# A recurrence on one core: gate products in every step of a six-step loop, two transposes for one, and convolutions without dependent pairs

## The reference, cut to what matters

```python
def cell(h, x):
    gi = x @ W_ih + b_ih
    gh = h @ W_hh + b_hh
    i_r, i_z, i_n = jnp.split(gi, 3, axis=-1)
    h_r, h_z, h_n = jnp.split(gh, 3, axis=-1)
    r = jax.nn.sigmoid(i_r + h_r)
    z = jax.nn.sigmoid(i_z + h_z)
    n = jnp.tanh(i_n + r * h_n)
    h_new = (1.0 - z) * n + z * h
...
x = x + attention(x, cond)
x = x + gru(cond, x)
x = x + conv(x, w)         # w is cond, 4 taps
x = x + (conv(x, w) + b)
```

## Time and profile before

| | |
|---|---|
| median of three runs | 2157.09 us (2156.23 to 2157.23) |
| the profiled execution | 2157.61 us, span 2155.8 us |
| TensorE, matrix products busy | 2077.1 us, 96% |
| VectorE busy | 1391.0 us, 65% |
| ScalarE busy | 1173.3 us, 54% |
| GpSimd busy | 619.1 us, 29% |
| mean granted TensorE clock | 0.997 of full speed |

### The profile page before, as it was taken

One profiled execution on the slowest core, in us unless ns is written; L12 is line 12 of the kernel. 1 busy time (PEld: TensorE's weight loads), 2 busy tenths in 40 slices (PEclk: granted clock), 3 DMA queues, 4 the chain that ended last, 5 costly groups with the idle time before them and its releaser, 6 DMA issues.

```text
span 2155.8 us, 174734 instructions
## 1 busy us (share of the span) xinstructions
PE 2077.1 (96%) x76072; PEld 1575.3 (73%) x76072; DVE 1391.0 (65%) x5136; ACT 1173.3 (54%) x5995; POOL 619.1 (29%) x885
## 2 busy tenths in 40 slices
PE   8999999999999999999999999999999999999997
PEld 2222222222499999999999999999999999998886
DVE  4344444444377777777777777777777777776776
ACT  3444544443255555555555555555555555555555
POOL 0355545444112222222222222222222222222222
PEclk9999999999999999999999999999999999999999
DMA  6000000011222121212222122222221212210001
GB/s 254 1 1 1 1 1 1 1 59 31 55 52 52 48 57 49 56 47 54 70 54 51 50 53 50 53 65 58 52 54 49 53 49 65 59 31 6 5 7 19
DMA packets 218062, 95.88 MB, mean 44 GB/s; under 512 B 170216, under 2 KB 213480, under 8 KB 217320
## 3 DMA queue, kind: packets, MB, share of 16 engines
q1 hardware_dynamic: 217032, 92.00, 16.4%
q10 hardware_dynamic: 928, 2.65, 0.3%
HBM read 26.30 MB, written 12.58 MB: 18 GB/s over the span
## 4 chain that ended last, share of the span: by engine, by line
PE 88%; DVE 10%; issue 1%; ACT 1%; DMA 0%; ACTq 0%; SPq 0%; DVEq 0%
PE ps L1210 56%; PE ps L596 14%; DVE arena L1039 5%; PE ps L1238 4%; PE ps L772 3%; PE ps L699 3%; PE ps L790 3%; PE ps L1249 2%; DVE arena L1051 2%; DVE arena L1045 1%; DVE arena L1056 1%; PE ps L802 1%; PE ps L775 1%; ACT arena L347 0%; DMA arena<-arena 0%
## 5 line engine op out<-in xcount | busy, mean ns | idle before, releaser
L1210 PE MATMUL ps<-whh,arena 128*4 128x128 f32 (+1 forms) x65536 | 1447.8, 246 | 49.9 <-DVE arena L1056 44.7
L1210 PEld LDWEIGHTS ps<-whh,arena 128*4 128x4 f32 x65536 | 1303.5, 87 | 152.6 <-DVE arena L1056 77.6
L1039 DVE STREAM_TRANSPOSE arena<-ps 128x128 f32<-128x128 f32 x1024 | 434.5, 424 | 233.7 <-PE ps L1210 232.8
L1168 ACT ACTIVATE arena<-arena 128x8 f32<-128x8 f32 x1024 | 216.0, 211 | 635.7 <-DVE arena L1039 627.8
L441 DVE TENSOR_REDUCE top<-ps 128x2 f32<-128x1024 f32 x128 | 150.8, 1220 | 256.3 <-PE ps L699 256.3
L1056 DVE TENSOR_TENSOR_SCAN arena<-arena 128x24 f32<-128x24 f32 x1024 | 213.1, 208 | 145.0 <-ACT arena L1179 145.0
L1143 ACT ACTIVATE ps<-arena 128x128 f32<-128x128 f32 x1026 | 269.6, 263 | 1.8 <-DMA arena<-arena 1.8
L1045 DVE STREAM_TRANSPOSE arena<-ps 128x64 f32<-128x64 f32 x1024 | 256.2, 250 | 13.0 <-PE ps L1210 3.4
L596 PE MATMUL ps<-arena 128*32 128x512 f32 x2048 | 242.4, 595 | 2.7 <-ACT arena L369 2.7
L347 ACT ACTIVATE arena<-ps 128x1024 f32<-128x1024 f32 x128 | 124.1, 1021 | 214.1 <-PE ps L775 214.0
L1179 ACT ACTIVATE arena<-arena 128x16 f32<-128x16 f32 x1024 | 222.9, 218 | 8.7 <-DVE arena L1051 0.9
(11 more groups left out here) (97 smaller groups left out, 1219.0 us busy)
## 6 DMA issues: line engine op xcount, KB each, us to landing
arena<-arena SPq DMA_DIRECT2D x216, 114.0 KB, 2.2
arena<-arena SPq DMA_DIRECT2D x112, 128.0 KB
arena<-seq SPq DMA_DIRECT2D x224, 55.0 KB
arena<-gi_d SPq DMA_DIRECT2D x248, 32.0 KB
gi_d<-arena SPq DMA_DIRECT2D x96, 57.0 KB, 2.3
out<-seq SPq DMA_DIRECT2D x14, 256.0 KB
seq<-in_x SPq DMA_DIRECT2D x3, 1024.0 KB, 15.7
whh<-in_w_hh SPq DMA_DIRECT2D x1, 3072.0 KB, 21.6
```

Source lines behind the costliest of these rows:

```text
L1039: e.transpose(trn[:, h].rearrange("p q (i c s) -> p q c i s", c=2, s=2)[:, :, :, :, 0], bank[RN[h]][:, 0:P].rearrange("p (q c i) -> p q c ...
L1168: e.activation(r_d0[:, h].rearrange("p (i s) -> p i s", s=2)[:, :, 1], trn[:, h, 0, 0:2 * NH].rearrange("p (i s) -> p i s", s=2)[:, :, 0], ...
L1210: last = e.matmul(bank[dst[h]][32 * G:32 * G + B, 0:n], hv, wv[:, k, gates, G, 64 * h:64 * h + 64], start=False, stop=k2 == 1 and k == C - ...
```

## The change

TensorE's gate loop is now six steps long and runs 72 times (432 steps), followed by 80 steps without gate products. AW becomes 86 (12 blocks in a row, 144 blocks) and NW 43 (72 blocks). The first four steps of a body are each followed by half of an r/z block, so a body has two of them, and the last two by half of an n block each. VectorE takes the r/z blocks out after steps 2 and 4, and the n block, now with its bias added in the same instruction, after step 0 of the next body; `seed_n` is gone. `turn_rn` becomes two transposes of 64 columns, r first, each counting `s_tr`, so the sigmoid of r waits for the first alone; the scan for n and ScalarE's next seed wait for the second. GpSimd's batch has 15 operations of single width, and those of one let-in don't depend on each other. The last batch's tail is shared: VectorE starts on it in tiles of its own while GpSimd ends the batch before.

```diff
-        AW, NW = 114, 55
+        AW, NW = 86, 43
...
-        BODIES = 2 * len(N_BLOCKS)
+        BODY = 6
+        BODIES = len(N_BLOCKS)
         NRZ = len(RZ_BLOCKS)
-        assert NRZ <= BODIES and 4 * BODIES <= T
+        assert NRZ == 2 * BODIES and BODY * BODIES <= T
...
-        n_fixed = tile([P, 2, P])
-        n_moving = tile([P, 2, CW])
+        n_fixed = tile([P, C, P])
+        n_moving = tile([P, C, CW])
...
-        NB, POOL_OPS, END_OPS = 8, 7, 13
+        NB, POOL_OPS, END_OPS = 8, 8, 15
...
-        def conv_halves(e):
-            return e.tensor_tensor(prd[:, 4 * wide:6 * wide], prd[:, 0:2 * wide], prd[:, 2 * wide:4 * wide], ALU.add)
+        def conv_add(e, dst, a, b, held=prd):
+            return e.tensor_tensor(conv_part(dst, held), conv_part(a, held), conv_part(b, held), ALU.add)
...
SyncE:
-                for q in range(T // 4):
-                    step = 4 * q
+                for step in range(0, T, 2):
                     if step % HALF == 0 and 0 < step < T - HALF:
                         next_half(step + HALF)
-                    if q < BODIES:
-                        if q + 1 < BODIES:
+                    body, u = divmod(step // 2, 3)
+                    if body < BODIES and u < 2:
+                        q = 2 * body + u
+                        if q + 1 < NRZ:
                             for v in range(2):
                                 e.wait_ge(st["s_rzpart"], 2 * q + v + 1)
                                 bring_rz(q + 1, v)
-                            e.wait_ge(st["s_npart"], q + 1)
-                            bring_n(q + 1)
-                        if q < NRZ:
-                            keep(q)
+                        keep(q)
+                    elif body + 1 < BODIES:
+                        for v in range(2):
+                            e.wait_ge(st["s_npart"], 2 * body + v + 1)
+                            bring_n(body + 1, v)
...
VectorE:
+                    n_at = (count(6 * t + 2), count(6 * t + 5))
...
                     def turn_rn(h):
                         e.wait_ge(st["s_rn"], half[h])
-                        e.transpose(trn[:, h].rearrange("p q (i c s) -> p q c i s", c=2, s=2)[:, :, :, :, 0],
-                                    bank[RN[h]][:, 0:P].rearrange("p (q c i) -> p q c i", q=2, c=2)
-                                    ).then_inc(st["s_tr"], 1)
+                        for q in range(2):
+                            e.transpose(trn[:, h, q].rearrange("p (i c s) -> p c i s", c=2, s=2)[:, :, :, 0],
+                                        bank[RN[h]][:, 64 * q:64 * q + 64].rearrange("p (c i) -> p c i", c=2)
+                                        ).then_inc(st["s_tr"], 1)
...
                     def scan_n(h):
+                        e.wait_ge(st["s_tr"], n_at[h])
                         e.wait_ge(st["s_sig"], half[h])
...
-                seed_n(0)
+                e.sem_inc(st["s_nfree"], 1)
                 for q in range(BODIES):
-                    for v in range(4):
-                        step(4 * q + v, v % 2)
-                        if v == 0 and q and q % 2 == 0:
-                            seed_n(q // 2)
-                        if v == 2:
-                            take_rz(q)
-                        if v == 3 and q % 2 == 1:
-                            take_n(q // 2)
-                with e.Fori(2 * BODIES, T // 2) as it:
+                    for v in range(BODY):
+                        step(BODY * q + v, v % 2)
+                        if v == 0 and q:
+                            take_n(q - 1)
+                        if v in (2, 4):
+                            take_rz(2 * q + v // 2 - 1)
+                take_n(BODIES - 1)
+                with e.Fori(BODY // 2 * BODIES, T // 2) as it:
...
ScalarE:
                         reset(0)
+                        e.wait_ge(st["s_tr"], turned[1])
                         seed_rn(0, s)
...
TensorE:
                 with e.Fori(0, BODIES) as it:
-                    for v in range(4):
-                        step(it * 4 + v, v % 2)
-                        if v < 2:
-                            part_rz(v, it)
-                        elif v == 2:
-                            part_n(it)
-                with e.Fori(2 * BODIES, T // 2) as it:
+                    for v in range(BODY):
+                        step(it * BODY + v, v % 2)
+                        if v < 4:
+                            part_rz(v % 2, e.snap(it * 2 + v // 2))
+                        else:
+                            part_n(v % 2, it)
+                with e.Fori(BODY // 2 * BODIES, T // 2) as it:
...
GpSimd, one batch (made(n) waits for the batch's own count):
+                    let_in(0)
+                    if finish:
+                        made(0)
+                        conv_add(e, 6, 6, 7)
+                    conv_product(e, seq, 0, t).then_inc(s, 1)
...
+                    let_in(3)
+                    made(3)
+                    conv_add(e, 4, 0, 1)
+                    conv_add(e, 5, 2, 3).then_inc(s, 1)
+                    let_in(4)
+                    made(4)
+                    e.tensor_tensor(seq2[:, :, bass.ds(t + PAD, NB)], conv_part(4), conv_part(5), ALU.add).then_inc(s, 1)
+                    let_in(5)
+                    made(5)
+                    conv_product(e, seq2, 0, t)
+                    conv_product(e, seq2, 1, t).then_inc(s, 1)
```

More of the change, by code:

```diff
@@ L971, in bring_rz, with bring_n @@
                     e.dma_start(a_moving[:, ks, :], wrz[:, ks, first:first + AW]).then_inc(s_apair[v], 16)
[L973 to L979, removed]
+                def bring_n(q, v):
+                    first, c, b = N_BLOCKS[q]
+                    ks = slice(2 * v, 2 * v + 2)
+                    e.dma_start(n_fixed[:, ks, :], wn[:, ks, P * c:P * c + P]).then_inc(s_npair[v], 16)
+                    for k in (2 * v, 2 * v + 1):
+                        e.dma_start(n_moving[:, k].rearrange("p (b t) -> p b t", b=2),
+                                    seq_cb[:, k, b:b + 2, PAD + first:PAD + first + NW]).then_inc(s_npair[v], 16)
                 def keep(q):
@@ L1240, in part_rz, with part_n @@
                     last.then_inc(st["s_rzpart"], 1)
-                def part_n(q):
-                    e.wait_ge(st["s_nseed"], e.snap(q + 1))
-                    e.wait_ge(st["s_npair"], e.snap(q * 48 + 48))
-                    for k in range(2):
+                def part_n(v, q):
+                    if v == 0:
+                        e.wait_ge(st["s_nfree"], e.snap(q + 1))
+                    e.wait_ge(s_npair[v], e.snap(q * 48 + 48))
+                    for k in (2 * v, 2 * v + 1):
                         for g in range(NG):
@@ L1272, in wait, with batch, made @@
                     e.sem_inc(s_apart, 1)
-                with e.Fori(0, T // NB - 1) as it:
-                    t = e.snap(it * NB)
+                def batch(it, t, finish):
                     def let_in(m):
                         wait(st["s_x3"], it * NB + NB + m)
+                    def made(n):
+                        wait(s, it * POOL_OPS + n)
                     let_in(0)
-                    conv_product(e, seq, 0, t)
-                    conv_product(e, seq, 1, t)
+                    if finish:
+                        made(0)
+                        conv_add(e, 6, 6, 7)
+                    conv_product(e, seq, 0, t).then_inc(s, 1)
@@ L1283, in _ @@
                     let_in(1)
+                    if finish:
+                        made(1)
+                        e.tensor_tensor(seq[:, :, bass.ds(t - NB, NB)], conv_part(6), conv_part(3), ALU.add)
+                    conv_product(e, seq, 1, t).then_inc(s, 1)
+                    let_in(2)
+                    made(2)
                     conv_product(e, seq, 2, t)
                     conv_product(e, seq, 3, t).then_inc(s, 1)
-                    let_in(2)
-                    wait(s, it * POOL_OPS + 1)
@@ new lines, in batch @@
+                    let_in(7)
+                    made(7)
+                    conv_product(e, seq2, 3, t)
+                    conv_add(e, 7, 1, 2).then_inc(s, 1)
+                batch(0, 0, False)
+                with e.Fori(1, T // NB - 1) as it:
+                    batch(it, e.snap(it * NB), True)
+                n = POOL_OPS * (T // NB - 1)
+                wait(st["s_x3"], T)
+                wait(s, n)
+                conv_add(e, 6, 6, 7).then_inc(s, 1)
+                wait(s, n + 1)
@@ L1308 @@
+                e.tensor_tensor(seq[:, :, T - 2 * NB:T - NB], conv_part(6), conv_part(3), ALU.add).then_inc(s, 1)
+                wait(s, n + 2)
 _INS = ['x', 'cond_2048', 'L0_cond_W_emb', 'L0_cond_b_emb', 'L0_cond_g_norm', 'L0_cond_W_qkv', 'L0_cond_g_q',
```

97 lines of the change are left out of this document (39 added, 58 removed).

## The result

The changed kernel takes 2270.9 us in the median (2270.1 to 2273.5, 6 runs) where the kernel before took 2156.0 beside it. The ratio is 1.0534 with a 95% interval of 1.0521 to 1.0548: 115 us slower. The forecast was 2264 us, 107 us slower, within 2225 to 2352. The total is right, and most of it for the stated reason. Two terms, the step with the split transposes and the branch back of the loop, were wrong and nearly cancelled each other.

A forecast was written before the change was run, and what follows sets the result against it. Two limits bind: TensorE's 3.03 us a step and the chain's 3.00. 72 bodies of 19.76 us (1423), 80 steps (244), less 3, plus 5, give 107 us more; with 0.5 at the end, 2264 us, within 2225 to 2352.

The forecast's parts named there:

- the chain: Dependent work from TensorE's start through the transposes to half 0's end scan and TensorE's next start: 3.00 us a step.
- It just makes it: State half 1 ends at P + 3.83, in time for its first product in the next step at 3.89.
- The wait for `take_rz`: At step 2 of each body TensorE waits for VectorE's `take_rz`: 4.51 us to step 3, 1.46 more than another step.
- Two transposes for one: End scan of half 0 stands behind both transposes of half 1: chain's limit 2.71 + 2s, 3.05 us a step.
- s: On VectorE, time from a transpose's start to the start of what follows: 0.17 us, upper bound 0.25.
- rival 2: TensorE's longer loop doesn't stay in instruction memory, one gap of 1.42 us per body: 102 us more, 2366 us; chance 0.06.
- rival 4: TensorE's clock might drop from idling 1.56 us in each sixth step; given nothing of its own.
- The end and the rest: VectorE's last batch adds 0.5 us; `take_n`, SyncE's queue and the extra waits cost little.
- its 5 us for the first body: Gaps in TensorE's issue in the first body, put in at 5 us (bounds 2 and 8).

The follow-up runs named there:

- take_early: The changed kernel with VectorE taking the r/z blocks out after steps 1 and 3 of a body instead of 2 and 4: 2156.6 us, ratio 1.000.
- experiment 3: Two transposes for one on the kernel before: 2151.0 us; one for two on take_early: 2170.4 us. With the split, ten to twelve gate steps take up to 0.37 us more.
- before_both: The kernel before, loop of four steps, with the new convolutions and the two transposes for one: 2145.5 us, ratio 0.9945.

## Why the prediction was right, and where it was not

- **What bounds the kernel before.** Held: TensorE at 3.03 us in gate steps, the chain near 3.00 without them, and GpSimd's dependent pairs: the convolutions without them gave 10.8 us alone. "It just makes it", of half 1, is true to 0.01 us for the matrix products: in the gate steps of the kernel before, the first one behind the wait starts 0.089 us after the one before, for 0.083 where nothing is waited for (behind the branch in take_early). The weight load does wait, 0.10 us in a typical step.
- **The wait for `take_rz`.** Right in place, count and mechanism. Forecast 1.46 us over an ordinary step, 72 times, 105 us; two independent ways to take it away gave 114 and 113 us back. Measured it is 4.61 - 2.97 = 1.64 us. 0.08 us of the difference are TensorE's start behind the wait and 0.03 the half block; the other 0.08 is that an ordinary step is shorter than I had it.
- **Two transposes for one.** This term failed, though the total came out. I had 3.05 us a step, 0.05 worse than today's limit. It is 2.97 to 2.98 in steps without a wait or a branch, and 3.02 with the whole transpose in the same loop (13.8 us more), so the split gains where I had a loss. The term was 2s + 0.21 = 0.55 us and measured 0.30 + 0.17 = 0.47. The second transpose starts 0.17 us after the first, as s had it; the scan starts 0.13 after the second, and takes 0.17 where I had kept 0.21. The rule about DRAIN (the Trainium skill, "VectorE: DVE Perf Modes", section "The DRAIN you can't avoid") would have needed each of them to start when the one before has ended. The transposes are recorded as 0.31 and 0.26 us, so the trace doesn't agree. But the same section adds that an operation that is not "held" starts earlier; I had left this out, and no run here shows which operations are held.
- **The branch back.** Missing from the sum: about 0.2 us, 72 times, and as much in 40 of the last 80 steps. The last 80 take 3.11 us for my 3.05. This made up for the steps that were faster. Counted from the starts of the matrix products, a body is 2.98 + 2.97 + 4.61 + 2.97 + 2.97 + 3.22 = 19.72 us, and 19.78 in the mean of all behind the first, with the delays of experiment 3; the forecast was 19.76. The first body takes 4.8 us more than a mean one, for 5 in the sum. That the bodies agree is luck: an ordinary step 0.08 us too long, five times, against a branch of about 0.2 us left out and a wait 0.10 us too short.
- **Instruction fetch (rival 2).** It did not happen in the changed kernel (49 packets). But 128 instructions further on it does, and costs 992 us, with 18 us for the empties, nearly ten times my 102: I took one gap a body, and every block of the loop is late. My reason against it, that 1728 records for 1120 is no doubling, was no reason. The Trainium skill, "Runtime: NRT & Kernel Launch", section "Instruction fetch mechanics", gives TensorE's memory as 2048 instructions. By that number the loop fits, at some 1750 instructions (an estimate: its 1728 records and the waits). Here it depends on its place whether it stays.
- **The clock (rival 4).** It did not come: the granted clock was 1.00 from 600 to 1950 us in the changed kernel, though TensorE idled 1.5 us in each body.
- **The end and the rest.** The time behind the last step grew from 7.7 to 8.5 us; I had 0.5 more. `take_n`, SyncE's queue and the added waits cost nothing that shows behind the first body: with the wait gone, five steps of six run at 2.97 to 3.00. In the first body an operand is late, by 2.26 us in the changed kernel; the sum had no such wait by name, but its 5 us for the first body hold it.
- **Where the change's gain went.** Without the wait the new loop's 512 steps take 1560.6 us for 1561.6. Over the gate steps, first bodies included, take_early needs (1903.0 - 587.8) / 432 = 3.04 us a step and the old loop with both other edits (before_both) (1946.5 - 587.8) / 448 = 3.03. The branch, uncovered, and a slower first body take back what the even spread gives.

## What to carry to other kernels

Before a loop is rearranged, write down for each single-buffered tile which instruction empties it and where this stands in its engine's order, relative to the next user's place in its own. Here two lines moved by one step decide over 114 us. A count that only says "emptied" is safe in any order, and hides such a stall. A loop that has grown, as here from 1120 to 1728 matrix records, should be tried at several places in the code, and the packets of its instruction queue read, before it is trusted.

## What the runs showed of the hardware that I had not expected

- The same loop of TensorE (1728 matrix records a round) stayed in place with 0 and 240 instructions ahead of it, and was fetched anew in each round, 9 packets of 16.4 KB, with 128: 31.8 us a round for 18.3. A loop of 1120 records stayed with 0 and with 128. Where exactly the limit lies is open: no run moved it in small steps.
- A branch back costs TensorE about 0.2 us where it has no idle time before the target. In a small loop 0.2 us are lost or not by where the code lies, behind the first matrix instruction of the loop, though the engine idles 0.3 us a step in both.
- 128 empty semaphore instructions on TensorE cost 18.3 us, 0.14 us each; 60 tiny matrix instructions (240 records with their weight loads) took 3.9 us.
- After 20.75 us without matrix work TensorE's granted clock was 0.50 and a step took 5.30 us for 2.83. With 1.5 us of idling in every 19.8 us it stayed at 1.00.
- VectorE starts a scan 0.30 us after the first of two 64-column transposes that last 0.43 us together.
